# First attention of a four-layer network: heads read back per image, last image's heads stored by SyncE, two images projected ahead

## The reference

```python
def _forward(x, qkv_w, proj_w, proj_b):
    ...
            outs.append(_dilate_attention(qkv[i, 0], qkv[i, 1], qkv[i, 2], hd, scale, KSZ, DILATIONS[i]))
    y = jnp.stack(outs).reshape(B, H, W, C)
    return y @ proj_w.T + proj_b
...
x = x + _L0_conv_ref(_ln_c(x), L0_conv_qkv_w, L0_conv_proj_w, L0_conv_proj_b)
t = _to_tokens(x)
t = t + _L0_ffn_ref(_ln_t(t), L0_ffn_Wg, L0_ffn_W1, L0_ffn_b1, L0_ffn_W2, L0_ffn_b2)
```

## Time and profile before

| | |
|---|---|
| runs | 813.16, 810.92, 805.61 us; median 810.92 |
| profiled execution | 812.87 us, its span 811.2 us |
| granted TensorE clock, mean | 0.889 |
| PE busy | 668.7 us (82%) |
| DVE, ACT, POOL busy | 387.0, 303.1, 229.2 us |
| first attention and its output projection | about 10 to 135 us |

### The profile page before, as it was taken

How to read it: one execution, slowest core, us unless ns; L and a number is a source line. 1 busy time by engine, 2 the same in 40 slices (tenths; PEclk the granted TensorE clock), 3 DMA queues, 4 the chain that set the end, 5 groups by cost and what they waited for, 6 DMA issues and landing times. The chain is left out here.

```text
span 811.2 us, 12856 instructions
## 1 busy us (share of the span) xinstructions
PE 668.7 (82%) x4034; PEld 556.4 (69%) x4034; DVE 387.0 (48%) x978; ACT 303.1 (37%) x604; POOL 229.2 (28%) x274
## 2 busy tenths in 40 slices
PE   4888936997996999957989983799995798898397
PEld 2476725685794899953677763699994367776296
DVE  4566816114445433314578756343440466885301
ACT  2344524232413344422434552235442243454222
POOL 5176620001200044442045400724334204541000
PEclk9989977798996899985899995899998589999599
DMA  3745720634206166533497503577653349840442
GB/s 90 195 114 142 176 57 0 156 99 96 48 1 175 40 161 160 121 48 65 131 248 212 111 17 113 149 177 183 170 124 48 70 132 233 222 114 1 102 119 72
DMA packets 92485, 95.14 MB, mean 117 GB/s; under 512 B 17313, under 2 KB 78644, under 8 KB 92424
## 3 DMA queue, kind: packets, MB, share of 16 engines
q1 hardware_dynamic: 78952, 74.91, 34.6%
q0 software_dynamic: 11808, 18.38, 11.3%
q10 hardware_dynamic: 1680, 1.28, 0.6%
HBM read 66.92 MB, written 27.84 MB: 117 GB/s over the span
## 5 line engine op out<-in xcount | busy, mean ns | idle before, releaser
L2017 POOL DMA_INDIRECT sum_scratch<-area,f_row_index x48 | 72.4, 1509 | 177.6 <-DVE area L1963 167.9
L881 DVE TENSOR_REDUCE neg_max<-psum 128x4 f32<-128x1024 f32 x72 | 87.9, 1221 | 31.0 <-PE psum L767 30.2
L1722 PE MATMUL psum<-w,area 128*112 128x192 f32 (+1 forms) x576 | 96.2, 326 | 0.0
L1722 PEld LDWEIGHTS psum<-w,area 128*112 128x112 f32 (+1 forms) x576 | 93.5, 183 | 0.0
L961 POOL TENSOR_TENSOR shift<-ident,neg_max 128x256 fp32r<-128x256 f32 x96 | 66.5, 704 | 84.8 <-DVE neg_max L881 56.4
L779 PE MATMUL psum<-q_parts,k_parts 128*128 128x256 f32 x288 | 78.5, 303 | 0.4
L780 PE MATMUL psum<-shift,ones_r 128*128 128x256 f32 x288 | 74.2, 289 | 0.0
L767 PE MATMUL psum<-k_parts,q_parts 128*128 128x256 f32 x288 | 52.9, 307 | 19.9 <-DVE neg_max L881 8.6
L1821 DVE TENSOR_TENSOR q_parts<-w,q_parts 128x1536 fp32r<-128x1536 f32 x16 | 28.1, 1758 | 82.7 <-ACT q_parts L1751 82.7
L779 PEld LDWEIGHTS psum<-q_parts,k_parts 128*128 128x128 f32 x288 | 56.7, 197 | 10.8 <-issue 8.2
L360 PE MATMUL psum<-ident,x_norm 128*96 128x128 f32 x128 | 26.1, 349 | 45.0 <-DVE x_norm L330 44.8
(11 more groups left out here) (250 smaller groups left out, 1328.9 us busy)
## 6 DMA issues: line engine op xcount, KB each, us to landing
w<-in_f_w_dram SPq DMA_DIRECT2D x32, 576.0 KB, 4.8
w<-in_f_w_dram SPq DMA_DIRECT2D x16, 384.0 KB, 4.4
w<-in_f_w_dram SPq DMA_DIRECT2D x32, 192.0 KB, 5.2
q_parts<-q_scratch SPq DMA_DIRECT2D x32, 192.0 KB, 3.6
q_scratch<-area SPq DMA_DIRECT2D x22, 192.0 KB, 2.1
k_parts<-k_scratch SPq DMA_DIRECT2D x63, 64.0 KB, 3.1
q_parts<-q_scratch SPq DMA_DIRECT2D x32, 96.0 KB, 2.9
q_parts<-q_scratch SPq DMA_DIRECT2D x40, 64.0 KB, 3.3
```

Of the source, the lines that this page charges most:

```text
L881: ins = dve.tensor_reduce(most, ps[:, 0:2, :].rearrange("p b (c k) -> p (b c) k", c=2), AX_X, ALU.max, negate=True)
L1722: ins = pe.matmul(ps[0:R, 6 + c // 2, D * (c % 2):D * (c % 2 + 1)], x.hidden[:, fc, R * c:R * (c + 1)], net.w2[:, b, fc, :], start=(fc == ...
L2017: pool.indirect_dma_start(net.sum_dram[:, :], bass.IndirectOffsetOnAxis(ap=row_index[0:size, b, c:c + 1], axis=0), x.y[0:size, b, c, :], N ...
```

## The change

- In layer 0 the heads are read back image by image (`reread_image`, 192 KB each, two tiles), each with a semaphore of its own. Images 0, 1 and 2 are reread inside the attention block: SP, after its loads, waits for POOL's stores of the image.
- The three quads of image 3 are stored by SP, not POOL, with a semaphore `last_stored`. POOL has no store, and no wait for stores, after its loop. In step 1 of an image POOL waits, before its store, until the stores of the image two before have landed.
- In the next block SP waits for `last_stored` and rereads image 3. PE turns and projects tiles 0 to 3 (images 0 and 1) first, and then waits for the rereads of images 2 and 3. Layers 2 and 3 keep their order.

```diff
@@ attention, sync @@
+            if m.local:
+                for i in range(IMGS - 1):
+                    sp.wait_ge(stored, DMA * GROUPS * (i + 1))
+                    reread_image(net, m, sp, i)
+                for g in range(GROUPS):
+                    store_heads(sp, IMGS - 1, g, m.last_stored)
@@ attention, gpsimd @@
                 if m.local and s % 2 == 1:
-                    store_heads(i - 1, s // 2)
+                    if s == 1:
+                        need(pool, stored, (i - 1) * (DMA * GROUPS))
+                    store_heads(pool, i - 1, s // 2, stored)
...
-            if m.local:
-                for g in range(GROUPS):
-                    store_heads(IMGS - 1, g)
-                pool.wait_ge(stored, DMA * IMGS * GROUPS)
@@ new @@
+def reread_image(net, m, eng, i):
+
+    src = net.o_dram[i].rearrange("n t c -> (n t c)").rearrange("(t p c) -> p t c", p=P, c=D)
+    eng.dma_start(net.mixed[:, 2 * i:2 * i + 2, :], src).then_inc(m.reread[i], DMA)
@@ attention_output, sync @@
             if m.local:
-
-                for q in range(2):
-                    src = net.o_dram[2 * q:2 * q + 2].rearrange("i n t c -> (i n t c)").rearrange(
-                        "(t p c) -> p t c", p=P, c=D)
-                    sp.dma_start(net.mixed[:, 4 * q:4 * q + 4, :], src).then_inc(reread, DMA)
+                sp.wait_ge(m.last_stored, DMA * GROUPS)
+                reread_image(net, m, sp, IMGS - 1)
@@ attention_output, tensor @@
+            turn_half(0)
+            if not m.local:
+                turn_half(1)
+            for b in (0, 1):
+                project(b)
+            if m.local:
+                turn_half(1)
+            for b in (2, 3):
+                project(b)
             norm.tensor(pe)
```

More of the change, by code:

```diff
@@ L504, in attention @@
     clipped, pad_exp, stored = sem(tag + "_clipped"), sem(tag + "_pad_exp"), sem(tag + "_stored")
+    if m.local:
+        m.last_stored = sem(tag + "_last_stored")
+        m.reread = [sem(f"{tag}_reread{i}") for i in range(IMGS)]
     kinds = 1 if m.local else 3
@@ L692, in attention, with store_heads @@
     rest_per_step = 2
+    def store_heads(eng, i, g, done):
+        eng.wait_ge(mixed_sb, i * GROUPS + (g + 1))
+        src = tiles_of(net.mixed, i).rearrange("p t c -> p (t c)")[
+            :, 2 * HD * GH * g:2 * HD * GH * (g + 1)].rearrange("p (n x) -> p n x", n=GH)
+        dst = net.o_dram[bass.ds(i, 1), group(g), :, :].rearrange("i n (p t) c -> p (i n) (t c)", t=2)
+        eng.dma_start(dst, src).then_inc(done, DMA)
     def shift_of(n, s, b):
@@ L947, in stage_v @@
                                           "p t (n x) -> p t n x", x=HD)).then_inc(v_set, 1)
[L949 to L954, removed]
             def shift(i, s):
@@ L1008, in tiles_of @@
     return buf[:, bass.ds(2 * i, 2), :]
+def reread_image(net, m, eng, i):
+    src = net.o_dram[i].rearrange("n t c -> (n t c)").rearrange("(t p c) -> p t c", p=P, c=D)
+    eng.dma_start(net.mixed[:, 2 * i:2 * i + 2, :], src).then_inc(m.reread[i], DMA)
 def attention_output(net, m, norm, start=()):
     nc, ps, tag = net.nc, net.psum, m.tag
-    reread = net.sem(tag + "_reread")
     turned = net.sem(tag + "_mix_turned")
@@ L1024, in _, with turn_half @@
             if m.local:
-                for q in range(2):
-                    src = net.o_dram[2 * q:2 * q + 2].rearrange("i n t c -> (i n t c)").rearrange(
-                        "(t p c) -> p t c", p=P, c=D)
-                    sp.dma_start(net.mixed[:, 4 * q:4 * q + 4, :], src).then_inc(reread, DMA)
+                sp.wait_ge(m.last_stored, DMA * GROUPS)
+                reread_image(net, m, sp, IMGS - 1)
         @block.tensor
         def _(pe):
-            for q in range(2):
+            def turn_half(q):
                 if m.local:
-                    pe.wait_ge(reread, 2 * DMA)
+                    for reread in m.reread[2 * q:2 * q + 2]:
+                        pe.wait_ge(reread, DMA)
                 for half in range(2):
@@ L1040, in _, with project @@
                     ins.then_inc(turned, 1)
-            for b in range(4):
+            def project(b):
                 pe.wait_ge(turned_sb, 2 * (b // 2) + 2)
```

## The result

The changed kernel takes 800.2 us (median of 20 runs), the one before 807.9 us in the runs beside it. The ratio is 0.9898 with a 95% interval of 0.9876 to 0.9920, that is 8.2 us (6.5 to 10.0) less. One of the 20 runs, 806.96 us, was in a slower state and is left out of the ratio; the two medians are 7.7 us apart. The forecast was 9.3 us less.

The account below looks back on a forecast made before the run. PE's 11.8 us wait for the reread, about 5 us of it POOL's block end, was the bound. An earlier start (5.3) plus half done and clock kept (4.0) gave 9.3 us: 810.92 to 801.6 us, range 796.5 to 807.8.

Parts of the forecast that it names:

- T0: When PE starts the output projection's block after the first attention: predicted at 110.1 us.
- T: When PE's second half (images 2 and 3) starts in the output projection: predicted at 114.6 us.
- M: Time from the first attention's last mixed heads to DVE's first feed-forward instruction: 16 to 17.5 us claimed.
- Part 1: First attention's block end: without its last stores and wait POOL drains by 106.6 us, so PE starts at 110.1 us.
- Part 2: SP's queue in the first attention: rereads of images 0 to 2 and POOL's new wait cost 0 us.
- Part 3: After the first attention: the last store lands after 2.1 us, the last reread after 2.9 us, at 114.2 us.
- The margin of 0.4 us: Output projection: the last reread lands at 114.2 us, PE is through with images 0 and 1 at 114.6 us.
- Part 4: Output projection: PE does images 0 and 1 in 4.5 us; DVE's feed-forward begins 11.56 us after the second half starts.
- the clock falls all the same: Rival, chance 0.10: TensorE's clock drops at the hand-over anyway, costing about 2.7 us; gain 6.6 us, ending at 804.3 us.
- the old 1.37 us: Output projection's tail before the change: 1.37 us longer than the third attention's, put down to TensorE's lower clock.
- The table rule: Rival, chance 0.05: ScalarE's table switch in the output projection costs 1.4 us beyond its row; gain 7.9 us, 803.0 us.
- The forecast case: Chance 0.70: the hand-over from first attention to feed-forward shortens by 9.3 us, ending at 801.6 us.

Follow-up runs that it names:

- e3: The change, but POOL stores the last image's heads after its loop without waiting for them to land; 805.89 us, 0.9948 of the kernel before.
- e6: The change plus ten unread transposes at the first attention's end and five in the next block; 798.96 us, 0.9890 of the kernel before.
- e5: The change with ScalarE's table load and first deviation moved between the copies of images 0, 1 and 2, 3; 800.43 us, 0.9901 of the kernel before.
- e9: The change plus only five unread transposes after the next block's first eight transposes; 798.93 us, one run.
- e7: The change with the edits of e5 and e6 together; 796.08 us, 0.9863 of the kernel before.
- e8: The change plus only ten unread transposes at the end of the first attention; 798.31 us, one run.

## Why the prediction was right, and where a term was off

- **Its own signs.** The prediction named what would show it wrong, and one of the signs came: the clock was at the lower level between T0 and T + 5 (112.6 to 116). M was to be 16 to 17.5 us and is 18.21. The other signs went its way: POOL's drain begins at 102.9, PE starts 1.00 us after the heads, there is no gap before the second transposes, and DVE stands 1.74 us for ScalarE's deviation. So three parts of the mechanism held and one did not.
- **Part 1 held.** T0 was to be 0.93 us after the heads and is 1.00. The reason given, that half of POOL's part was its drain and not the wait, was argued from the third attention; e3 shows it by itself.
- **Part 2 held.** The rereads of images 0 to 2 and the new wait on POOL cost nothing: the last heads come at 109.28 against 109.17. SP got past the wait for image 2 at 105.41, predicted 105.3.
- **Part 3 held with room.** Store and reread landed after 1.8 and 2.4 us, taken as 2.1 and 2.9. The margin of 0.4 us became 2.9, since PE asked late.
- **Part 4, the step that failed: "PE is through with images 0 and 1 at T0 + 4.5".** It was T0 + 6.15. The first half ran partly at the lower clock: 4.55 us where 2.74 were set. That is the rival "the clock falls all the same", which I gave 0.10 because PE resumes before the time of the old fall; it resumed at 110.28 and the clock fell at 112.6 all the same. Its price was put at 2.7 us. The 1.7 us for the stretched first matmuls came (4.55 against 2.87); the old 1.37 us did not come on top, because the clock was back at 116, before the second half. In e6, without the fall, the second transposes are 1.7 us earlier and M is 1.25 us shorter. Of the rest of the chain the terms were right: third sum at T + 4.23 (4.3), because of ScalarE's table load (e5), and DVE's next block at T + 11.06 (11.56). The 0.5 us there are mostly the clock again: it stayed up until 126.3, and the last eight transposes of the norm were 0.42 us shorter than those of the third attention, from which the term was taken (its row, then that of the change):

```profile
751.35 1.94 PE L360 MATMUL psum<-ident,x_norm 128*96 128x128 f32 x8 [1.52 <-DVE x_norm L330]
125.11 1.52 PE L360 MATMUL psum<-ident,x_norm 128*96 128x128 f32 x8 [1.52 <-DVE x_norm L330]
```

- **The table rule.** ScalarE's load stands at 118.16, 0.02 us after its second copy's end (117.07 + 1.07), and is over at 119.44, 0.12 us before the deviations' row at 119.56: the row's 1.28 us is all that it cost. The drain of about 1.38 us that the Trainium skill adds for a switch (ScalarE: Activation LUTs, What ACT_TABLE_LOAD costs) does not show here, neither before the load nor behind it.
- **The sum.** 9.3 us minus 1.7 for the clock plus 0.5 at the end is 8.1, the measured gain in M. The forecast case and its first rival were both half true, and they lay close together (9.3 and 6.6 us), which is why the range held. The range of 796.5 to 807.8 us would have held a gain of 3.1 us as well, and the 3.4 us that it adds above 804.4 come from no row.
- **The level.** The median of three runs that I started from, 810.92, was 3 us above that of twenty, 807.9. From 807.9 the forecast gain would have given 798.6, and 800.2 was measured. That 801.6 came within 1.4 us is partly luck: the level was put too high and the gain too large, and the two errors work against each other.

## What to carry to other kernels

Ask of a block's end which engine drains last, not only which waits last: moving the last stores from POOL to SP took 3.4 us off a barrier whose wait was already gone. When work is pulled ahead of a wait, follow every engine's program order behind it: here a table load and a normalisation queued behind the late half gave back 0.9 us. And a hole that is made shorter (10.7 to 1.0 us here) does not by itself keep the clock up; a few unread transposes did in all four kernels that had them. Before such a gain is claimed for the whole kernel, look at when the clock comes back in the next block: that alone moved W by up to 1 us.

## What the runs showed of the hardware that was not expected

- POOL's drain at the end of an attention's block takes 2.6 to 2.8 us once POOL's work is done (a row of 3.7 to 3.8 us where it starts while POOL still works, in e3 and the change), and 0.05 us at the end of the output projection's block, where POOL has nothing. It is not one price for every block in which POOL worked: behind the 5.1 us sum of the Fourier mixer it was 0.2 us before and 0.9 us with the change. SP's takes 0.12 us with transfers of its own still under way.
- Five transposes (0.71 us) behind a stand of 2 us and eight transposes kept the granted clock at 1.0 where without unread transposes it fell to 0.5 within 3.6 to 4.7 us (1.7 once) of the attention's last matmul (one profile, e9).
- The clock's return in the feed-forward block came 18.3 to 21.2 us after the block's start, and the changed kernels' block length followed it, 54.9 to 56.2 us. The two latest returns (e6 and e7, 1.7 and 1.9 us after that of the change) held the clock up in the projection, but so did the earliest (e8, 1.0 us before it), so it is not shown that the one causes the other; why the return scatters is open.
